# A two-layer transformer kernel: who mixes, gates and writes out the last batch

## The reference, cut to what matters

```
q, k        = xn @ Wq, xn @ Wk                        # 8 heads of 64
src, dst    = top-2-of-5 of xn @ Ws, of xn @ Wd       # per token and head
XV[n, e]    = xn @ Wv[e]                              # 5 experts of 64 = 320 numbers
V[n, h]     = sum_e  WV[n, h, e] * XV[n, e]           # "mixing": WV = sigmoid * chosen(src)
A[n, h]     = softmax(q k^T) V                        # per head
G[n, e]     = sum_h  MO[n, h, e] * A[n, h]            # "gating": MO = chosen(dst), 0 or 1
x           = x + G @ Wo                              # 320 -> 256
```

## Time and profile before

| What | Value |
| --- | --- |
| median of 3 executions | 2807.13 us (2803.64 to 2812.64) |
| the profiled execution, its own time | 2811.8 us |
| its span, first to last instruction | 2810.1 us |
| PE busy over the span | 2339.5 us (83%) |
| DVE busy | 1902.4 us (68%) |
| POOL busy | 1862.9 us (66%) |
| ACT busy | 1673.5 us (60%) |
| mean granted TensorE clock | 0.88 |

### The profile page before, as it was taken

The page is one execution under the profiler, slowest core; times in us unless marked ns, Lnnn a source line. Parts: engine busy times, 40 slices in busy tenths (PEclk is TensorE's granted clock), DMA queues, the critical chain, the costliest instruction groups (busy, mean ns, idle before and its releaser), DMA issues. The chain is left out here.

```text
span 2810.1 us, 31463 instructions
## 1 busy us (share of the span) xinstructions
PE 2339.5 (83%) x10169; PEld 1174.3 (42%) x10169; DVE 1902.4 (68%) x3134; ACT 1673.5 (60%) x2352; POOL 1862.9 (66%) x1858
## 2 busy tenths in 40 slices
PE   5667777787777777775888799999999999999985
PEld 2222323232323323233555455555555555555543
DVE  5787989898988988763333356565756666666655
ACT  1778888889788888980122255555555555555440
POOL 0555587787878787873577302958585858595866
PEclk8667787878778787786899899999999999999997
DMA  3000000000000010114799500000000000000000
GB/s 104 16 1 1 17 16 16 18 16 18 9 25 8 10 23 3 30 15 107 218 265 226 112 1 1 1 1 23 1 23 1 23 1 20 4 8 1 9 0 16
DMA packets 94052, 98.97 MB, mean 35 GB/s; under 512 B 18848, under 2 KB 90656, under 8 KB 93856
## 3 DMA queue, kind: packets, MB, share of 16 engines
q1 hardware_dynamic: 70704, 73.99, 9.1%
q0 software_dynamic: 23152, 22.68, 4.6%
HBM read 69.98 MB, written 26.66 MB: 34 GB/s over the span
## 5 line engine op out<-in xcount | busy, mean ns | idle before, releaser
L1049 POOL TENSOR_TENSOR TT<-TT,SS 128x512 f32<-128x512 f32 x512 | 652.0, 1309 | 223.8 <-ACT SS L978 223.3
L1791 ACT ACTIVATE PR<-S,NM 128x512 f32<-128x512 f32 x512 | 345.3, 686 | 260.2 <-DVE NM L1958 260.2
L1958 DVE TENSOR_REDUCE NM<-S 128x2 f32<-128x1024 f32 x256 | 301.7, 1220 | 131.7 <-PE S L1685 131.7
L734 DVE TENSOR_SCALAR TT<-SC 128x1024 f32<-128x1024 f32 x256 | 311.6, 1217 | 75.4 <-POOL TT L1049 44.6
L464 PE MATMUL OB<-TT,VAL 128*17 128x512 f32 x1024 | 345.3, 777 | 4.6 <-ACT TT L986 4.6
L736 DVE SCALAR_TENSOR_TENSOR SS<-SC,TT 128x1024 f32<-128x1024 f32 x256 | 313.6, 1225 | 20.6 <-issue 1.8
L1054 POOL DMA_INDIRECT slot_tokens<-TID,IDX x224 | 229.3, 1024 | 101.1 <-issue 67.1
L1696 PE MATMUL TP<-ident,PR 128*128 128x128 f32 x2048 | 273.3, 276 | 21.2 <-DVE TT L1963 18.2
L1696 PEld LDWEIGHTS TP<-ident,PR 128*128 128x128 f32 x2048 | 235.0, 142 | 113.7 <-issue 66.9
L1963 DVE COPY TT<-TP 128x512 f32<-128x512 f32 x256 | 176.3, 689 | 151.4 <-PE TP L1696 147.6
L1797 ACT ACTIVATE TT<-TP 128x512 f32<-128x512 f32 x256 | 153.3, 599 | 195.1 <-PE TP L1696 191.3
(11 more groups left out here) (293 smaller groups left out, 4083.9 us busy)
## 6 DMA issues: line engine op xcount, KB each, us to landing
TT<-w_gu SPq DMA_DIRECT2D x64, 384.0 KB
TT<-w_dn SPq DMA_DIRECT2D x64, 128.0 KB
XL<-x SPq DMA_DIRECT2D x8, 512.0 KB
stream<-V SPq DMA_DIRECT2D x4, 1024.0 KB, 10.3
rows<-XL SPq DMA_DIRECT2D x8, 512.0 KB
TT<-w_dn SPq DMA_DIRECT2D x64, 64.0 KB
XS<-stream SPq DMA_DIRECT2D x8, 512.0 KB, 4.3
out<-XS SPq DMA_DIRECT2D x8, 512.0 KB, 2.9
```

Of the source, the lines that this page charges most:

```text
L734: dve.tensor_scalar(tt[:, :, mt, :], SC[mt % 2][:], 0.0, None, ALU.max)
L1049: ins = pool.tensor_tensor(tt, tt, ss, ALU.add)
L1791: act.activation(PR[s % 2][h2][:], S[s % 2][:, h2, :], ACT.Exp, bias=NM[:, s % 2, h2:h2 + 1], accum_out=SM[:, pair % 2, j, h2:h2 + 1]).the ...
L1958: dve.tensor_reduce(NM[:, s % 2, :], S[s % 2][:], AX, ALU.max, negate=True).then_inc(sems["peak"], 1)
```

## The change

In the last batch and just before it, work moves between engines and places:
- POOL mixes only the even head of each pair. DVE forms the odd head in two operations: `weigh_own` multiplies all five experts' values (1280 elements) into VW, `sum_own` reduces over the experts into VN. Attend waits for both.
- ACT multiplies the even heads of the gating (`own_gate`, 80 operations of 64 elements with a scale per token, in eight halves of ten); DVE adds them up (`own_sum`). POOL keeps the odd heads.
- `heads2` of the third pair goes before the tail's first attend instead of behind it.
- Batch 6's `turn_out2` is copied by ACT and one or two slots later; its third and fourth products go into the tail.
- The end of batch 7 goes by token tile: `join`, `turn_last` (three turns, one copy by ACT), `product_last`, the add and a store of 128 KB for each of the four tiles, instead of one join, three chunks, four products and one store of 512 KB.
- POOL's adds of 1280 elements become four of 320. This holds for all batches (L2092) as well as the last (L2071).

```diff
@@ -1290,7 +1290,9 @@
     (0, 7, D3, "sigmoid", 0), (0, 7, D3, "choose", 3), (0, 7, D3, "choose", 4), (0, 7, C3, "experts", 1),
     (1, 0, A, "experts", 2), (1, 0, Z, "experts", 3), (1, 0, D3, "choose", 5), (1, 0, D3, "choose", 6), (1, 0, D3, "mix_values", 0),
     (1, 0, C3, "queries2", 1), (1, 1, A, "keys2", 1), (1, 1, C3, "queries2", 2), (1, 2, A, "keys2", 2), (1, 2, Z, "queries2", 3),
-    (1, 2, C3, "keys2", 3), (1, 2, D3, "mix_values", 1), (1, 4, D3, "mix_values", 2), (1, 5, D3, "mix_values", 3))
+    (1, 2, C3, "keys2", 3), (1, 2, D3, "mix_values", 1), (1, 4, D3, "mix_values", 2), (1, 5, D3, "mix_values", 3),
+    (1, 1, A, "weigh_own", 0), (1, 1, D3, "sum_own", 0), (1, 2, A, "weigh_own", 1), (1, 2, Z, "sum_own", 1),
+    (1, 2, D3, "weigh_own", 2), (1, 3, D3, "sum_own", 2), (1, 4, D3, "weigh_own", 3), (1, 5, D3, "sum_own", 3))
 NORM_1 = table((0, 7, D3, "stats", 0))
 NORM_1_LATE = table((0, 6, D3, "stats", 0))
 PREP_1 = table(
@@ -1307,12 +1309,12 @@
 OUT_2_LAST = table((0, 0, Z, "turn_out2", 0), (0, 0, C3, "turn_out2", 1), (0, 1, C3, "turn_out2", 2),
                    (0, 3, C3, "product_out2", 0), (0, 4, A, "product_out2", 1), (0, 4, C3, "product_out2", 2),
                    (0, 5, A, "product_out2", 3))
-OUT_2_LATE = table((0, 5, C3, "turn_out2", 0), (0, 6, A, "turn_out2", 1), (0, 6, C3, "turn_out2", 2),
-                   (0, 7, A, "product_out2", 0), (0, 7, Z, "product_out2", 1), (0, 7, C3, "product_out2", 2),
-                   (1, 0, 1, "product_out2", 3))
-OUT_2_TAIL = table((0, 4, 3, "join", 0), (0, 4, 3, "turn_out2", 0), (0, 4, 3, "turn_out2", 1), (0, 4, 3, "turn_out2", 2),
-                   (0, 4, 4, "product_out2", 0), (0, 4, 4, "product_out2", 1), (0, 4, 4, "product_out2", 2),
-                   (0, 4, 4, "product_out2", 3))
+OUT_2_LATE = table((0, 6, A, "turn_out2", 0), (0, 6, C3, "turn_out2", 1), (0, 7, A, "turn_out2", 2),
+                   (0, 7, Z, "product_out2", 0), (0, 7, C3, "product_out2", 1),
+                   (1, 3, 2, "product_out2", 2), (1, 4, 3, "product_out2", 3))
+OUT_2_TAIL = table((0, 4, 4, "join", 0), (0, 4, 4, "turn_last", 0), (0, 4, 4, "join", 1), (0, 4, 4, "turn_last", 1),
+                   (0, 4, 4, "product_last", 0), (0, 4, 4, "join", 2), (0, 4, 4, "turn_last", 2), (0, 4, 4, "product_last", 1),
+                   (0, 4, 4, "join", 3), (0, 4, 4, "turn_last", 3), (0, 4, 4, "product_last", 2), (0, 4, 4, "product_last", 3))
 HEADS_1 = table((0, 3, Z, "spread", 0), (0, 5, Z, "spread", 1), (0, 7, Z, "spread", 2), (1, 1, Z, "spread", 3),
                 (0, 3, D3, "heads1", 0), (0, 5, D3, "heads1", 1), (0, 7, D3, "heads1", 2), (1, 1, D3, "heads1", 3))
 SET_DOWN = table((0, 3, D3, "set_down", 0), (0, 5, D3, "set_down", 1), (0, 7, D3, "set_down", 2))
@@ -1325,8 +1327,11 @@
     (0, 4, Z, "heads2", 0), (0, 6, Z, "heads2", 1), (1, 1, Z, "heads2", 2), (1, 3, Z, "heads2", 3),
     (0, 5, D3, "gate", 0), (0, 6, D3, "gate", 1), (1, 1, D3, "gate", 2), (1, 3, D3, "gate", 3))
 HEADS_2_TAIL = SET_DOWN + table(
-    (1, 3, 2, "set_down", 3), (0, 4, Z, "heads2", 0), (0, 6, Z, "heads2", 1), (1, 0, 2, "heads2", 2), (1, 4, 2, "heads2", 3),
-    (0, 5, D3, "gate", 0), (0, 6, D3, "gate", 1), (1, 0, 3, "gate", 2), (1, 4, 3, "gate", 3))
+    (1, 3, 2, "set_down", 3), (0, 4, Z, "heads2", 0), (0, 6, Z, "heads2", 1), (1, 0, 1, "heads2", 2), (1, 4, 2, "heads2", 3),
+    (0, 5, D3, "gate", 0), (0, 6, D3, "gate", 1), (1, 0, 3, "gate", 2), (1, 4, 3, "gate", 3),
+    (0, 4, D3, "own_gate", 0), (0, 5, D3, "own_gate", 1), (0, 6, D3, "own_gate", 2), (0, 7, D3, "own_gate", 3),
+    (1, 0, 3, "own_gate", 4), (1, 0, 3, "own_gate", 5), (1, 4, 3, "own_gate", 6), (1, 4, 3, "own_gate", 7),
+    (1, 0, 2, "own_sum", 1), (1, 4, 3, "own_sum", 2), (1, 4, 3, "own_sum", 3))
 
 
 def timetable():
...
@@ -1442,6 +1448,12 @@
     FIRST = table((0, 0, 3, "absorb", 0), (0, 0, 3, "stats_first", 0), *[(0, 0, 3, "turn_norm", c) for c in range(DC)],
                   (0, 0, 3, "latent", 0), (0, 0, 3, "queries1", 0))
 
+    def turned_bank(j):
+        return S[j // 2][:, j % 2]
+
+    def made_bank(j):
+        return (TP[0][:], TP[1][:], OT[:], S[0][:, 0])[j]
+
     def reader(part, i):
         return READER[part][i]
 
...
@@ -1482,13 +1494,16 @@
                 sp.dma_start(X[b][:], x_b[b]).then_inc(sems[f"x_in{b}"], 16)
             for dst, src in loads_later:
                 sp.dma_start(dst, src).then_inc(sems["weights_later"], 16)
-            for b in range(B):
+            for b in range(B - 1):
                 sp.wait_ge(sems["x4"], b + 1)
                 sp.dma_start(out_b[b], X[b % XN_RING][:]).then_inc(sems["out_st"], 16)
                 if b + XN_RING < B:
                     sp.wait_ge(sems["out_st"], 16 * (b + 1))
                     sp.dma_start(X[b % XN_RING][:], x_b[b + XN_RING]).then_inc(sems[f"x_in{b % XN_RING}"], 16)
-            sp.wait_ge(sems["out_st"], 16 * B)
+            for j in range(NT):
+                sp.wait_ge(sems["out_last"], j + 1)
+                sp.dma_start(out_b[B - 1, :, j, :], X[(B - 1) % XN_RING][:, j, :]).then_inc(sems["out_st"], 16)
+            sp.wait_ge(sems["out_st"], 16 * (B - 1 + NT))
 
         @block.tensor
         def _(pe):
...
+                if c == 0:
                     pe.wait_ge(sems["gadd"], v.next("gadd", H1))
                 lo = min(c * P, SV - P)
                 for j in range(NT):
-                    ins = pe.transpose(bank[:, j * P:(j + 1) * P], (GL_POOL if last else GO)[:, j, lo:lo + P], ident[:])
-                ins.then_inc(sems["item_d"], 1)
+                    ins = pe.transpose(bank[:, j * P:(j + 1) * P], GO[:, j, lo:lo + P], ident[:])
+                ins.then_inc(sems["item_" + way], 1)
+
+            def turn_last(v, j, b):
+                pe.wait_ge(sems["joined"], j + 1)
+                for c in range(3):
+                    lo = min(c * P, SV - P)
+                    ins = pe.transpose(turned_bank(j)[:, c * P:(c + 1) * P], GL_POOL[:, j, lo:lo + P], ident[:])
+                ins.then_inc(sems["turned_last"], 1)
+
+            def product_last(v, j, b):
+                pe.wait_ge(sems["taken_last"], j + 1)
+                for c in range(3):
+                    ins = pe.matmul(made_bank(j)[:, 0:D], AT2[:, c, j * P:(j + 1) * P], o2[:, c, :],
+                                    start=(c == 0), stop=(c == 2))
+                ins.then_inc(sems["made_last"], 1)
 
             def product_out2(v, j, b):
-                bank = free_bank(3 + j) if b == B - 1 else item(v, "free_d")
-                if b == B - 1 and v.all_due("free_d"):
-                    pe.wait_ge(sems["free_d"], v.value + 3)
+                bank = item(v, "free_d")
                 for c in range(3):
                     ins = pe.matmul(bank[:, 0:D], AT2[:, c, j * P:(j + 1) * P], o2[:, c, :],
                                     start=(c == 0), stop=(c == 2))
...
+                    if kind == 2 and b < B - 1:
                         pe.wait_ge(sems["vh"], v.next("vh", 2))
+                    elif kind == 2:
+                        pe.wait_ge(sems["vh"], H1 * b + pair + 1)
+                        pe.wait_ge(sems["vh_own"], pair + 1)
                 if kind == 1 and pair == 0 and m == 0:
                     need(v, "values1", b, 0)
                 for h2 in range(2):
...
+                act.wait_ge(sems["item_a"], v.next("item_a"))
+                act.activation(AT2[:, c, :], BK[:], ACT.Copy).then_inc(sems["free_a"], 1)
+
+            def own_gate(v, i, b):
+
+                pair, h = i // 2, i - i % 2
+                if i % 2 == 0:
+                    act.wait_ge(sems["head"], PAIRS1 * b + pair + 1)
+                    if pair >= 2:
+                        act.wait_ge(sems["own"], pair - 1)
+                dst = (GT_OWN if pair else GL_OWN).rearrange("p j (e d) -> p j e d", e=SE)
+                for j in range(NT // 2 * (i % 2), NT // 2 * (i % 2) + NT // 2):
+                    for e in range(SE):
+                        ins = act.activation(dst[:, j, e, :], AH[pair % 2][:, j, 0, :], ACT.Copy, scale=MO[b % 2][:, j, h, e:e + 1])
+                ins.then_inc(sems["own_mul"], 1)
+
+            def turn_last(v, j, b):
+                act.wait_ge(sems["turned_last"], j + 1)
+                act.activation(AT2[:, :, j * P:(j + 1) * P], turned_bank(j)[:, 0:3 * P].rearrange("p (c n) -> p c n", c=3), ACT.Copy)\
+                   .then_inc(sems["taken_last"], 1)
+
             def spread(v, pair, b):
                 act.wait_ge(sems["item_a"], v.next("item_a"))
                 act.activation(RBT[:], BK[:], ACT.Copy).then_inc(sems["spread_in"], 1)
...
-                    return
-                gl = GL_DVE.rearrange("p j (e d) -> p j e d", e=SE)
-                gt = GT_DVE.rearrange("p j (e d) -> p j e d", e=SE)
-                h = 2 * pair
-                dve.drain()
-                for j in range(NT):
```

(55 more changed lines are left out.)

34 lines of the change are left out of this document (15 added, 19 removed).

## The result

The kernel after takes 2798.6 us (median of 14 executions, 2792.2 to 2808.5), the kernel before on the same chips 2806.8 (14 executions, 2800.7 to 2812.6). The ratio is 0.9968, 95% interval 0.9960 to 0.9975: about 9 us faster, clear of the measurement's uncertainty, and a third of the 25.6 us that the prediction summed.

The account below looks back on a forecast made before the run. It took POOL's queue to set the end up to the last join, then a serial tail. Terms -19.6, +0.2, -4.9, -3.5 and +2.2 summed to -25.6, taking the median from 2807.1 to 2781.5 us; range 2770 to 2800.

Parts of the forecast that it names:

- The split adds of the other batches: POOL's adds in four pieces before the last batch: -4.9 for TensorE stalls, -3.5 for choosing comparisons, +2.2 loss.
- (a): In four batches a tiny DVE operation waits beside POOL's long add and TensorE idles behind it; these stalls vanish, -4.9.
- (b): Early in the third stage, five longer adds ahead in POOL's queue delay the normed tile TensorE awaits: +2.2, bounds 0 and 2.9.
- The last batch, -19.6: Walk of DVE, ACT and POOL with shared mixing: the last join starts at 2773.4 against 2793.0.
- -3.5: Run before the last: choosing comparisons no longer wait for POOL's long add, nor TensorE behind them; bounds 0 and -6.5.
- the set-down: TensorE's 7.1 us wait for a late DVE set-down in the last batch: covered by POOL, gives nothing of its own.
- The tail: Last batch's end by token tile: chain 14.8 against 13.7, smaller store -0.9, together +0.2; 2.9 more if products stay cold.
- D: Rival: gain mostly lost as POOL's mixing waits for DVE in the last batch and TensorE cools; 2797 to 2805, chance 0.11.
- A: The forecast as summed, 2781.5 us; chance 0.47.
- B: Rival: DVE and ACT fill the loop, multiplications 0.35, reductions 2.5, cold products; 2793.6 in full, about 2791; chance 0.23.
- C: Rival: more gained, by ACT's multiplications at 0.15, the choosing jam wholly gone, POOL's pieces free; 2772.3, chance 0.14.
- E: Rival: slower, ACT's multiplications at 0.85 each stand ahead of the turned copies; 2818.7, chance 0.05.

Follow-up runs that it names:

- experiment 3: The kernel after with POOL's adds of 1280 elements whole in all seven batches before the last: 2795.9 us.
- experiment 1: The kernel after with those adds whole in the first six batches, in four pieces only in the seventh: 2788.0 us, 0.9931 of before.
- experiment 2: The kernel before with one edit, the adds of 1280 elements in four pieces in all seven batches: 2819.5 us.

## Why the prediction was right and wrong

**The step that failed: "The split adds of the other batches".** It named both effects and mis-sized both. (a) "With pieces of 0.87 all four vanish: -4.9". They did vanish. But a stall is worth its length only if nothing else was about to be late. In before TensorE's turn at 1977.13 came 1.53 late, and POOL's normed tile was ready at 1982.6 for a turn at 1983.3, 0.7 us of slack, all of it bought by that stall. Without it TensorE would have wanted the tile at 1981.8. (b) "Loss: early in the stage TensorE waits 5.31 for POOL's normed tile", with five of these adds ahead of it, +2.2: counted once. The same five adds stand ahead of the second norm in four more batches, because the merge holds POOL's queue for 6.1 to 6.7 us there. Each tile came 2.1 us later (five adds, 0.42 each) against a demand 1.0 to 1.5 us sooner: waits of 3.27, 2.79, 2.82 and 2.77. Then the clock fell behind two of them. In place of -2.7 stands +10.5 (means of profiles); by the times, whole adds in these batches give back 10.4 (0.9968 against 0.9931). What is late next where a stall goes was walked for the last batch and not for the early ones. The signs that the prediction had named for this step came true (L1908 at 0.48 at most, 7.44 before the first normed tile); none of them looked at the second norm's tile.

**The last batch, -19.6 with -3.5.** The mechanism was right: the mixing halved, POOL not last, the chain DVE, ACT, DVE last by 1.8 us (2 forecast), the set-down worth nothing of its own. The size was -18.6 for both together, 4.5 short. Mis-sized: sum_own, 2.37 where 1.5 was taken (inside the bounds), twice ahead of copies; and the clock, which the walk kept at full speed between stalls. How the 4.5 divide between the two no run shows. Measured by profiles, the halves of the sum were -10.4 (experiment 3 against before) and -9.5 (experiment 1 against 3; 7.9 by the medians), not -19.6 and -3.5. That two errors of opposite sign leave 4.5 is luck. They can't be added as independent: experiment 2 shows the second at -2 without the first.

**Terms that held.** ACT's multiplications, 0.25 for 0.23. The estimate from the figures of the Trainium skill (ScalarE: Activation LUTs, "ACT is a hardware spline evaluator") was 0.24, and the trace agrees with 0.244 to 0.25. Four pieces 3.32 for 2.90, +0.42. A weight of 1280 beside POOL's pieces costs POOL 1.25 (4.57 for 3.32), 1.1 taken. The reductions cost POOL nothing: beside the sum at 2737.76 its mixing kept 0.62 and 0.72. The Trainium skill (SBUF — State Buffer, "Who interferes with whom") has tensor_reduce never contend with GpSimd on trn2, and the trace agrees. The tail, -0.3 for +0.2: in two of three profiles product 1 was at full clock, which the prediction had cold, and in the third products 1 and 2 were cold.

**The rivals.** The 2798.6 lies just inside the stated 2770 to 2800, and within the 2797 to 2805 of D; neither is to the prediction's credit, since A had 2781.5. D's mechanism wasn't what happened: POOL took the gain by its longer queue in the early batches, not by contention with DVE in the last. Of B the reductions at 2.4 came, the multiplications at 0.35 didn't, and its 2791 to 2793.6 was too low. C's multiplications at 0.15 and free pieces didn't come, nor did E's 0.85 per multiplication.

**Where the expected gain went:** 13 of the missing 17 us into waits for POOL's normed tile and the cold matmuls behind them, and the rest into the last batch's longer sums and colder matmuls.

## What to carry to other kernels

Two engines that are late in step hide each other. Before counting a stall as a gain, look when every other input of the waiting instruction is ready, and subtract that; the gain is the difference, not the stall. When an operation is made longer on an engine with a full queue, count it in every period, and find in the trace the one consumer with the least slack. Cut such a change to where it pays: splitting the adds of the seventh batch gave 8 us, splitting those of the other six as well cost 10.

A part with stalls near 2 to 3 us on TensorE needs several profiles of each kernel, since the clock decides differently each time. A filler ahead of a serial tail kept that tail at full clock in the one profile taken of it.

## What was not expected of the hardware

- **POOL issues a DMA at the price of its queue.** The merge took 1.34 us, and POOL's next operation came 5.34 later; over the four such merges of before and of after it was 4.7 to 5.3. The three merges at the stage's start stand 0.8 to 0.9 apart, so it is the next computing operation that comes late, not the next issue. In the page's row it isn't busy time.
- **DVE pays for a stride on either side.** 1280 elements: reduced in 1.49 when contiguous, 2.38 at a stride of 64 elements; multiplied in 1.49 to 2.09 when written in order, 2.48 to 3.07 at a stride of five.
- **The same program, the same stalls, another clock.** Behind a wait of 2.82 eight turns took 1.09 us in one execution and 1.97 in another; over the last batch the spread was 8 us in three profiles.
